# Second feed-forward of a two-layer gated cross-attention kernel: tokens sorted by expert group into eight tiles, with results scattered back

## The reference, cut to what matters

```python
shared = _swiglu(flat @ W_shared_in) @ W_shared_out        # 256 -> 2*512 -> 512 -> 256
g_probs = softmax(flat @ Wg_gate + group_bias)             # 2 groups
g_idx = argmax(g_probs)                                    # one group per token
e_probs = softmax(where(in_group, e_logits, -inf))         # 4 of the 8 experts
topv, topi = top_k(e_probs * g_prob, 2)                    # w: two nonzero weights of 8
h = _swiglu(flat @ W1_shared)                              # one hidden row for all experts
for e in range(8):
    routed = routed + h @ W2_experts[e] * w[:, e:e+1]      # 512 -> 256 each
out = _rmsnorm(x + shared + routed, norm2_w)
```

## Time and profile before

| | us |
|---|---|
| median of 3 runs | 583.16 |
| lowest and highest | 581.89, 585.56 |
| the profiled execution, its own time | 584.23 |
| its span in the trace | 582.4 |
| TensorE busy | 532.8 |
| VectorE, ScalarE, GpSimd busy | 282.0, 183.7, 125.6 |

### The profile page before, as it was taken

The page is one execution under the profiler, slowest core; times in us unless marked ns, Lnnn a source line. Parts: engine busy times, 40 slices in busy tenths (PEclk is TensorE's granted clock), DMA queues, the critical chain, the costliest instruction groups (busy, mean ns, idle before and its releaser), DMA issues. The chain is left out here.

```text
span 582.4 us, 9223 instructions
## 1 busy us (share of the span) xinstructions
PE 532.8 (91%) x3429; PEld 345.9 (59%) x3429; DVE 282.0 (48%) x660; ACT 183.7 (32%) x438; POOL 125.6 (22%) x146
## 2 busy tenths in 40 slices
PE   0989899899999879999999899999889999999995
PEld 0736575355556567788877677878535544544442
DVE  3436553121235575665676968887625222224242
ACT  1134331211103344555555545656532110000000
POOL 3112005001117252232232635341000000000000
PEclk9999968999999988999999999999989999999998
DMA  7989942279976697595573056000012000000000
GB/s 211 237 227 322 392 181 58 74 273 378 400 250 202 165 257 186 138 236 166 134 183 81 2 190 246 2 2 1 1 52 62 1 1 0 1 0 29 0 19 9
DMA packets 47087, 78.15 MB, mean 134 GB/s; under 512 B 6867, under 2 KB 36543, under 8 KB 46941
## 3 DMA queue, kind: packets, MB, share of 16 engines
q1 hardware_dynamic: 43841, 68.32, 38.0%
q0 software_dynamic: 3200, 9.22, 4.9%
HBM read 63.97 MB, written 12.13 MB: 131 GB/s over the span
## 5 line engine op out<-in xcount | busy, mean ns | idle before, releaser
L1392 PE MATMUL pb<-ring,big 128*128 128x512 f32 (+2 forms) x320 | 108.7, 593 | 2.3 <-DVE big L1343 1.2
L1392 PE MATMUL pb<-split 128*100 128x362 f32 (+2 forms) x320 | 78.3, 329 | 6.7 <-DVE nmx L1184 2.7
L1392 PEld LDWEIGHTS pb<-ring,big 128*128 128x128 f32 (+2 forms) x320 | 44.1, 166 | 59.4 <-issue 54.9
L1184 DVE TENSOR_REDUCE nmx<-pb 100x1 f32<-100x361 f32 x128 | 62.7, 527 | 25.6 <-PE pb L1392 25.2
L1392 PEld LDWEIGHTS pb<-split 128*100 128x100 f32 (+2 forms) x320 | 55.9, 183 | 16.7 <-issue 6.1
L860 ACT ACTIVATE big<-pb 121x400 f32<-121x400 f32 (+1 forms) x96 | 48.2, 505 | 23.9 <-PE pb L1392 21.6
L1364 DVE SCALAR_TENSOR_TENSOR ctxbuf<-pb,ctxbuf 128x256 f32<-128x256 f32 x48 | 23.2, 484 | 55.5 <-PE pb L1392 54.6
L1392 PE MATMUL pb<-big,arena 121*32 121x100 f32 (+3 forms) x1072 | 47.9, 264 | 1.5 <-ACT arena L710 1.2
L1392 PE MATMUL pb<-hT,ring 128*128 128x400 f32 x128 | 43.8, 501 | 0.5 <-DVE big L1343 0.5
L637 POOL TENSOR_TENSOR shift<-consts,nmx 100x400 fp32r<-100x400 f32 x32 | 28.3, 884 | 64.6 <-DVE nmx L1184 64.5
L1392 PE MATMUL pb<-hT,wgu 128*128 128x400 f32 (+2 forms) x108 | 39.7, 516 | 0.9 <-ACT hT L919 0.6
(11 more groups left out here) (242 smaller groups left out, 784.7 us busy)
## 6 DMA issues: line engine op xcount, KB each, us to landing
ring<-in_L_ffn_gate_up_proj SPq DMA_DIRECT2D x12, 1024.0 KB, 9.6
split<-kx_dram SPq DMA_DIRECT2D x64, 181.0 KB, 3.8
ring<-in_L_ffn_down_proj SPq DMA_DIRECT2D x12, 512.0 KB, 7.3
kx_dram<-split POOLq DMA_DIRECT2D x16, 362.0 KB, 4.9
ctxbuf<-in_L_ffn_gate_up_proj SPq DMA_DIRECT2D x4, 1024.0 KB, 9.6
ring<-in_L_ffn_W_experts SPq DMA_DIRECT2D x4, 1024.0 KB, 11.4
split<-qx_dram SPq DMA_DIRECT2D x64, 50.0 KB, 2.0
ctxbuf<-in_ctxT SPq DMA_DIRECT2D x6, 361.0 KB
```

The lines of the kernel that those rows point to most:

```text
L1184: nc.vector.tensor_reduce(nmx[:, t % 4, q:q + 1], PB[SB[n % 3]][0:T, 0:CTX], AX.X, ALU.max, negate=True) \
L1392: return nc.tensor.matmul(o, l, r, start=start, stop=stop)
```

## The change

Tokens are sorted by their group. `ET` = 116 rows make a tile, eight tiles make `NS` = 928 slots. Group 0 fills slots from the front, group 1 from the back, so no tile holds both groups. The core of the diff, by engine:

```diff
+ET = 116
+NS = NX * ET
+EX = D + 1 + 2 + NX
+FPARTS = [(0, 3), (3, 6), (6, 7), (7, 8)]
+W1_BANKS = [(2, 3), (4, 5), (6, 7)]
...
@@ sync, in the loop over items of the second cross-attention
                 if b == 3:
                     sp.wait_ge(s("filled"), FILL["values"])
+                    for i in range(NX):
+                        sp.dma_start(es_dram[ET * i:ET * i + ET, :], zero_rows[0:ET, :]).then_inc(s("b_zero"), 16)
+                        for d in (ex_dram, eb_dram):
+                            sp.dma_start(d[ET * i:ET * i + ET, :], zero_rows[0:ET, 0:D]).then_inc(s("b_zero"), 16)
                     sp.dma_start(wq2, A["L1_ffn_Wq"].rearrange("(k p) n -> p k n", p=128)).then_inc(s("ld_wd"), 16)
@@ sync, second feed-forward
-            for done, count, src, dst in (("n_hN", NB * (turn("e") + 1), hN, hF), ("c_res", NB, x, xF)):
...
-                    sp.dma_start(dst[at:at + n, c, :], src[row:row + n, b, :]).then_inc(s("ld_F"), 16)
...
-                sp.dma_start(flat_out[STARTS[c]:STARTS[c] + n], xF[0:n, c, :]).then_inc(s("stored"), 16)
+            sp.wait_ge(s("b_scat"), 2 * 16 * NB)
+            for g in range(NX // 2):
+                sp.dma_start(sorted_rows[0:ET, 2 * g:2 * g + 2, :],
+                             es_dram[2 * ET * g:2 * ET * (g + 1), :].rearrange("(i p) d -> p i d", p=ET)).then_inc(s(f"b_xg{g}"), 16)
+            sp.wait_ge(s("e_xst"), 16 * NB)
+            sp.dma_start(xF[0:ET], ex_dram.rearrange("(i p) d -> p i d", p=ET)).then_inc(s("ld_F"), 16)
+            sp.wait_ge(s("e_bst"), 16 * NB)
+            sp.wait_ge(s("n_tp"), NB // 2 * (turn("e") + 1) + NX // 2)
+            sp.dma_start(hF[0:ET], eb_dram.rearrange("(i p) d -> p i d", p=ET)).then_inc(s("ld_F"), 16)
+            sp.wait_ge(s("stored"), 16 * NX)
@@ gpsimd
+            for b in range(NB):
+                nc.gpsimd.indirect_dma_start(es_dram, bass.IndirectOffsetOnAxis(slot[:, b:b + 1], 0), stage(b), None, ...)
...
+                nc.gpsimd.indirect_dma_start(ex_dram, ..., x[:, b, :], ...).then_inc(s("e_xst"), 16)
...
+                pool.wait_ge(s("e_base"), b + 1)
+                nc.gpsimd.indirect_dma_start(eb_dram, ..., hN[:, b, :], ...).then_inc(s("e_bst"), 16)
...
+            for part, (a, z) in enumerate(FPARTS):
+                inverse_root("f", stdF, rstdF, only=part)
+                for i in range(a, z):
+                    pool.wait_ge(s("f_out"), i + 1)
+                    nc.gpsimd.indirect_dma_start(flat_out, bass.IndirectOffsetOnAxis(tok[0:ET, i:i + 1], 0), xF[0:ET, i, :], None, ...)
@@ vector
+            link(nc.vector.tensor_tensor(nflag, glT[:, :, 0], glT[:, :, 1], ALU.is_ge))
+            nc.vector.tensor_reduce(nsum, nflag, AX.X, ALU.add).then_inc(s("b_oh"), 1)
...
+            nc.vector.tensor_copy(slot[:], nslot).then_inc(s("b_slot"), 1)
...
+            for b in range(NB):
+                dve.wait_ge(s("e_down"), b + 1)
+                nc.vector.tensor_tensor(hN[:, b, :], PB[b][0:T, 0:D], stage(b)[:, 0:D], ALU.add).then_inc(s("e_base"), 1)
+            for g in range(NX // 2):
+                dve.wait_ge(s(f"b_xg{g}"), 32)
...
+            for i in range(NX):
+                for p in range(2):
+                    v = 2 * i + p
+                    dve.wait_ge(s("e_down"), NB + v + 1)
...
@@ tensor
+            for b in range(NB):
+                pe.wait_ge(s("n_hT"), NB // 2 * turn("e") + b // 2 + 1)
                 for k in range(KT):
-                    last = mm(PB[2 + half][0:2 + NX, 0:HALF], wge[:, k, :], hT[:, k, HALF * half:HALF * (half + 1)],
+                    last = mm(PB[4][0:T, (2 + NX) * b:(2 + NX) * (b + 1)], hT[:, k, T * b:T * b + T], wge[:, k, :],
...
+            shared_unit(0)
+            pe.wait_ge(s("b_oh"), 2)
+            mm(PB[5][0:T, 0:NB], consts[0:T, cs["lower"]], nflag, True, False)
+            for d in range(1, NB):
+                mm(PB[5][0:T, d:NB], ones[0:T, 0:T], nflag[:, 0:NB - d], False, d == NB - 1)
+            mm(PB[5][0:T, NB:NB + 1], ones[0:T, 0:T], nsum, True, True).then_inc(s("b_pos"), 1)
+            shared_unit(1)
+            pe.wait_ge(s("b_slot"), 3)
+            for u in range(2, 2 * FT):
+                shared_unit(u)
+            for b in range(NB):
...
+                for f in range(FT):
+                    last = mm(PB[b][0:T, 0:D], hidS[:, f, T * b:T * b + T], wdn[:, f, :], f == 0, f == FT - 1)
+            for g in range(NX // 2):
+                pe.wait_ge(s(f"b_xg{g}"), 32)
...
+                        last = nc.tensor.transpose(PB[g % 2][:, at:at + ET], sorted_rows[0:ET, 2 * g + q, 128 * k:128 * k + 128],
+                                                   ident[0:ET, 0:ET])
+            for u in range(2 * FT, 4 * FT):
...
+                if u < 2 * FT + 3:
+                    pe.wait_ge(s("e_base"), NB)
+                else:
+                    pe.wait_ge(s("e_hid"), u - 2)
...
+                        last = mm(PB[W1_BANKS[u % 3][w]][:, 0:4 * ET], wgu2[:, 1, k, F * w + 128 * f:F * w + 128 * f + 128],
+                                  hTs[:, k, 4 * ET * half:4 * ET * (half + 1)], k == 0, k == KT - 1)
+            first = [pe.value_load(offs[0:1, i:i + 1], min_val=0, max_val=EPG * D) for i in range(NX)]
             pe.wait_ge(s("e_hid"), 4 * FT)
+            for i in range(NX):
+                for p in range(2):
...
+                    for f in range(FT):
+                        last = mm(PB[v % 8][0:ET, :], hidE[:, f, ET * i:ET * i + ET], w2n[:, f, bass.ds(first[i] + 2 * D * p, 2 * D)],
+                                  f == 0, f == FT - 1)
```

More of the change, by code:

```diff
@@ L136, in values_read @@
     return max(read_out(p)[1] for p in VS[b])
[L139 removed]
+CONSTS = dict(ident=128, headmask=8, lower=T, cos=T, sin=T, rev16=NE, base16=NE, rev8=NX, token=NB, tiles=NX)
 def const_slices():
@@ L335, in build @@
         LN_PARTS = dict(a=[(0, NB)], b=[(0, NB - 2), (NB - 2, NB)], c=[(0, NB // 2), (NB // 2, NB)], d=UNITS,
-                        e=[(0, NB - 2), (NB - 2, NB)], f=PARTS)
-        FILL = {n: i + 1 for i, n in enumerate(("ones", "pads", "rows", "values", "pads_again", "queries", "sums"))}
+                        e=[(0, NB - 2), (NB - 2, NB)], f=FPARTS)
+        FILL = {n: i + 1 for i, n in enumerate(("ones", "pads", "rows", "values", "pads_again", "queries"))}
         def roots(st, part):
@@ L920, in _ @@
                     .then_inc(s("n_hT"), 1)
[L921 to L930, removed]
-            act.wait_ge(s("lg"), 2)
-            for u in range(4 * FT):
+            for u in range(2 * FT):
                 act.wait_ge(s("e_gu"), u + 1)
@@ new lines, in _ @@
+            dve.wait_ge(s("b_pos"), 3)
+            link(nc.vector.tensor_tensor(nslot, PB[5][0:T, 0:NB], nleft, ALU.add))
+            nc.vector.tensor_copy(slot[:], nslot).then_inc(s("b_slot"), 1)
+            link(nc.vector.tensor_tensor(oflag, consts[0:1, cs["tiles"]], PB[5][0:1, NB:NB + 1].to_broadcast([1, NX]), ALU.is_ge))
+            link(nc.vector.tensor_scalar(oflag, oflag, float(EPG * D), None, ALU.mult))
+            nc.vector.tensor_copy(offs[:], oflag).then_inc(s("b_slot"), 1)
+            for u in range(2 * FT):
+                half, f = u // FT, u % FT
+                dve.wait_ge(s("e_sil"), u + 1)
+                nc.vector.tensor_tensor(hidS[:, f, HALF * half:HALF * (half + 1)], sil[:, u % 2, 0:HALF],
+                                        PB[(2 * u + 1) % 8][:, 0:HALF], ALU.mult).then_inc(s("e_hid"), 1)
@@ L1392, in mm, with ln_pe @@
                 return nc.tensor.matmul(o, l, r, start=start, stop=stop)
-            def ln_pe(st, groups=range(NB // 2)):
+            def ln_pe(st, groups=range(NB // 2), row=lambda b: hN[:, b, :]):
                 for g in groups:
@@ L1828, in _, with shared_unit @@
             bank6_part("Y", NB - 1, 0)
-            ln_pe("e")
-            pe.wait_ge(s("n_hT"), NB // 2 * (turn("e") + 1))
-            for half in range(2):
+            ln_pe("e", row=stage)
+            for b in range(NB):
+                pe.wait_ge(s("n_hT"), NB // 2 * turn("e") + b // 2 + 1)
                 for k in range(KT):
-                    last = mm(PB[2 + half][0:2 + NX, 0:HALF], wge[:, k, :], hT[:, k, HALF * half:HALF * (half + 1)],
+                    last = mm(PB[4][0:T, (2 + NX) * b:(2 + NX) * (b + 1)], hT[:, k, T * b:T * b + T], wge[:, k, :],
                               k == 0, k == KT - 1)
-                last.then_inc(s("lgT"), 1)
-            def e_gu(u):
-                which, f, half = u // (2 * FT), u // 2 % FT, u % 2
+            last.then_inc(s("lg"), 1)
+            def shared_unit(u):
+                half, f = u // FT, u % FT
                 if u >= 4:
@@ new lines, in _ @@
+            for u in range(2 * FT, 4 * FT):
+                half, f = u // FT - 2, u % FT
+                if f == 0:
+                    pe.wait_ge(s("n_hT"), NB // 2 * (turn("e") + 1) + 2 * (half + 1))
+                if u < 2 * FT + 3:
+                    pe.wait_ge(s("e_base"), NB)
+                else:
```

(6 more changed lines are left out.)

222 lines of the change are left out of this document (103 added, 119 removed).

## The result

The changed kernel takes 597.37 us (median of 4, 595.63 to 600.43), the kernel before 582.52 (median of 4, 580.39 to 585.56). The ratio is 1.0256, with a 95% interval of 1.019 to 1.0323: slower by 2.6%. The interval is clear of no change, and its lower end is 1.9%. The forecast was 588.0, the range 572 to 600. The profiled execution has a span of 596.7 us, 14.3 above the 582.4 of before.

A forecast was written before the change was run, and what follows sets the result against it. The prediction took TensorE to bound the kernel, busy 532.8 of 582.4 us. 582.4 - 18.9 for the stage + 24 for the fills gave a 587.5 span, forecast as 588 us, range 572 to 600.

The forecast's parts named there:

- the forecast case: Whole kernel without the rivals: stage gain and fill stall nearly cancel, 8-in-10 range 579 to 598 us, chance 0.79.
- The zero fills, 24 us: SyncE's queue from 248.1: 116-row fills on 4 engines delay item 4's queries, stalling TensorE; 24 us, between 18 and 31.
- 0.91 "less a tenth": DMA share of the 128-row store in the earlier profile, less a tenth, read as 16 engines in use.
- The rival of 16 engines: Zero fills use all 16 engines, queries 4 to 12 us late, 570 us in all; chance 0.12.
- The stage up to TensorE's end, 130.4 us from 425.4: New second feed-forward, logits through second matrices: TensorE ends at 555.8; with the tail, 18.9 us less span.
- slot counting: Second feed-forward: 18 passes of at most 8 columns on TensorE, 2.6 us, between 2.2 and 3.4.
- the units: Second feed-forward, units 0 to 7: 64 passes, 21.7 us, and 1.6 for their first 3 us at half clock.
- The tail, 7.7 us: From TensorE's end to the span's end: 6.3 us now, 1.1 more for the indirect DMA, 0.3 for the wait.
- an indirect DMA after 2.8: Tail: a GpSimd-started indirect DMA lands after 2.8 us, where the present store lands 1.7 after issue.
- Register loads and register addresses at nothing: Second matrices: eight register loads cost nothing (4 us if exposed), passes with a register address stay at 0.434 us.
- The rival at 604: Second matrices: matmuls with a register address are slow, 0.25 us extra per product, 604 us in all; chance 0.05.
- Gating chain hidden, sorted rows in time: Second feed-forward: VectorE's 8 us chain is covered by transposes and three units; sorted rows ready near 463, needed near 471.

The follow-up runs named there:

- the kernel with the transposes behind `[3, 4, 5, 6]`: Kernel with all edits, its four groups of sorted-row transposes moved behind the fourth to seventh token blocks instead of second, fourth, sixth, seventh: 563.5 us.
- the fills made harmless: Changed kernel with its zero fills as 128-row transfers, issued after the loop over items: 570.0 us, ratio 0.9775 to the kernel before.
- the first attempts: Sorted-row transposes moved earlier, against the kernel with wide, moved fills: 568.6 us alone, 567.5 us with three more edits.

## Why the prediction was right and where it was off

The mechanism of the fills and of the stage was right, that of the tail was not priced right, and the sum was 9 us short. The range held the result (597.4 in 572 to 600), the forecast case's own range, 579 to 598, only just. The direction was hardly called: the forecast was 5 us slower with 0.43 each for "slower" and "same", and 14.9 were measured in the medians. By its steps:

- **The zero fills, 24 us: 27.2.** Four engines, the held queue, the stall from 269.8 and the restart at half clock are as forecast; the idle time ended at 294.4, forecast 292. The fills drained earlier than I had it (last one issued at 276.4; at 95 GB/s, not 77 to 89), but what came behind them landed later. The chain of waits of the kernel after has, where I had counted 2.0 us for the landing of the queries:

```profile
285.06 6.63 DMA split<-kx_dram
291.70 2.67 issue
```

  TensorE went on 5.2 us after the last query had been issued (289.2). The rule for the number of engines held, but one reading under it did not: 0.91 "less a tenth" is 13 engines and not 16. The 128-row fills of the experiment show the 16, with shares of 0.95 to 1.07 between 244 and 252.

  The rival of 16 engines falls by the share of 0.27. The kernel with wide fills is that rival made real: it forecast a stall of 4 to 12 us and 570 us in all, and 7.1 us and 579.0 were measured. It had taken 17 us of issue at worst, and 14.1 were needed.
- **The stage up to TensorE's end, 130.4 us from 425.4: 132.6** (452.71 to 585.3). Too large were the logits, 6.1 for 5.2 measured, slot counting, 2.6 for 1.7 (under its own bound of 2.2), the shared matrix, 14.0 for 13.8 (eight passes in 1.83, as the prediction reads them, would even make 14.6), and the second matrices, 55.5 for 55.2: 2.2 us in all. Too small were the units, 23.3 for 24.4, since unit 0 ran at half clock throughout; the transposes, 2.6 for 4.6, since I saw no hole between them; `W1_shared`, 25.1 for 26.3, behind a hole with the clock down (0.50 at 502 to 504); and the wait before the second matrices, 1.2 for 1.4: 4.4 us in all. That the sum is only 2.2 off is in part luck.
- **The tail, 7.7 us: 11.4.** This term was missed by the largest part of itself. The step that failed is "an indirect DMA after 2.8", from the earlier trace rows, with 0.3 for the wait. The landing of these scatters can be read in the trace of the kernel with the transposes behind `[3, 4, 5, 6]` (its line 720):

```profile
DMA to landing us min/median/max: 3.6/4.3/4.5
```

  It counts from the start of GpSimd's instruction. So a scatter of finished rows lands after 4.3 us, not 2.8 (1.5 more); GpSimd starts 1.3 us after VectorE's last operation, not 0.3 (1.0 more); and in that trace, where the last scatter starts at 552.9 and the span ends at 559.5, about 2.3 us follow the landing, where the kernel before has 0.9 behind a store that lands after 1.7 (1.4 more, and not in the sum at all). The start was 0.2 too high: the tail before was 6.1 us, not 6.3. Together that is the 3.7. The other scatter by token in the trace of the kernel before, in the first feed-forward, would have been no better source: it lands after 2.3 / 5.9 / 7.6 us (min, median, max). The Trainium skill ("DMA: Bandwidth & Descriptors", section on the anatomy of one DMA) fits a GpSimd transfer as 2.0 us and its bytes at 436 GB/s, which for 119 KB is an estimate of 2.3 us; the trace shows 4.3 to the landing of this scatter, and the measurement decides.
- **Register loads and register addresses at nothing:** right; 0.431 us for a pass either way, and 570.6 against 570.0 us without them. The rival at 604 falls.
- **Gating chain hidden, sorted rows in time:** right in the kernel after; transposes began as the shared matrix ended, and VectorE, which waits for all four loads of sorted rows, read them at 498.4. The chain was a near thing. It took 13.2 us (498.4 to 511.6) where I had counted 8, as it waits 5.1 us for ScalarE's exponential, which has a table load of 1.28 us before and behind it. VectorE came to the first product of `W1_shared` at 511.6, and ScalarE found the third unit done at 513.2; the fourth needs that product. In the kernel with the 116-row fills moved TensorE did wait for it, 0.73 us.

The sum by the measured terms: 587.5 + 3.2 + 2.2 + 3.7 = 596.6, the span is 596.7. And the counterfactual holds: with the fills made harmless the change is worth 582.4 - 569.5 = 12.9 us of span, which is the 18.2 of the stage less the 5.3 of the tail.

## What to carry to other kernels

Before a transfer goes into SyncE's queue in mid-kernel, ask for its row count's largest divisor up to 16 and for what is queued behind it: a side job of 2.9 MB cost more than the whole stage gained, and moved by 66 us, otherwise unchanged, it was free. A step that replaces a plain store at the very end by a scatter is priced from the last operation's end to the end of the span: the start of the issuing engine, the landing of that very kind of scatter, and what follows the landing. Like scatters of one trace landed after medians of 2.8 and 5.9 us, and this one after 4.3. When a hole on the busiest engine is filled by moving work forward, look at what the moved work waits for: the first attempts here traded one hole for another, and later in the order the same instructions cost no wait, in a trace in which the late Silu was absent too.

## What the hardware showed that I had not expected

- The number of engines that a transfer uses goes with its row count, and two rows make a difference: share 0.27 and 92 to 97 GB/s at 116 rows, 0.41 and 139 to 146 at 114.
- Full-width fills at the old place still cost 8 to 9 us in the median and 7.1 us of stall in the trace, of which their 14.1 us of issues, 4.8 above the slack of 9.3, explain the larger part. The loads behind them found busy engines (0.93 at 264 to 268).
- An indirect transfer of 116 rows of 1 KB took 6.5 us from the start of GpSimd's instruction to the end of the span (4.3 of them to the landing where the trace shows it), a plain one of the same bytes 3.9 from the start of its issue (559.77 to 563.7).
- ScalarE's Silu of unit 7 started 4.6 to 6.3 us after the one before it had ended, instead of 2.2, in the kernel after and in four of the experiments, with no recorded releaser. It came after 3.3 us in two, 2.5 in two, and on time in the last two. It matters only where TensorE waits for what follows it. Its cause was not found.
